# A depthwise convolution and a spiral scan on one core: PSUM seeded by ScalarE, half of the final updates split over ScalarE and GpSimd

## What is computed

```python
# layer 0
h = relu(x)
h = depthwise_conv3x3(h, dilation=2, SAME) + dw_bias
h = h @ pw + pw_bias                      # 256 -> 256
h = h * inv + (beta - moving_mean * inv)  # inv = gamma * rsqrt(var + 0.001)
# layer 1: one scan over the 3136 points of a spiral, from the centre outwards
for ci, neighbours in spiral:
    local = g[:, ci]
    neigh = mean of the (up to 4) neighbours' current values
    y = tanh(concat(local, neigh) @ w1 + b1) @ w2 + b2     # 512 hidden units, one scalar per image
    g[:, ci] = local + y * w_y
```

## Time and profile before

| | us |
|---|---|
| median of three runs | 4998.29 |
| the profiled execution, its own time | 5006.68 |
| its span | 5004.8 |
| PE busy | 4586.7 (92%) |
| DVE busy | 4012.3 (80%) |
| POOL busy | 3523.9 (70%) |
| ACT busy | 2289.1 (46%) |

### The profile page before, as it was taken

The page is one execution under the profiler, slowest core; times in us unless marked ns, Lnnn a source line. Parts: engine busy times, 40 slices in busy tenths (PEclk is TensorE's granted clock), DMA queues, the critical chain, the costliest instruction groups (busy, mean ns, idle before and its releaser), DMA issues.

```text
span 5004.8 us, 62963 instructions
## 1 busy us (share of the span) xinstructions
PE 4586.7 (92%) x20107; PEld 3278.7 (66%) x20107; DVE 4012.3 (80%) x6122; ACT 2289.1 (46%) x3670; POOL 3523.9 (70%) x2480
## 2 busy tenths in 40 slices
PE   3999999999999999999999999988888888887865
PEld 2778888888888888888888887744444444444432
DVE  6888888888887888888888888288888887877753
ACT  2555555555555555555555554343444443333321
POOL 3888888888887888888888888565666655554321
PEclk7999999999999999999999999999999999999985
DMA  3344344434444444343444342499998988876530
GB/s 92 112 131 138 128 138 128 138 128 138 128 138 131 135 128 138 128 138 128 138 128 138 128 138 106 173 315 295 295 313 285 285 271 253 242 222 188 168 108 25
DMA packets 395138, 835.35 MB, mean 167 GB/s; under 512 B 76864, under 2 KB 178496, under 8 KB 394688
## 3 DMA queue, kind: packets, MB, share of 16 engines
q1 hardware_dynamic: 251408, 420.08, 30.5%
q0 software_dynamic: 143408, 411.26, 22.0%
HBM read 419.95 MB, written 425.85 MB: 169 GB/s over the span
## 4 chain that ended last, share of the span: by engine, by line
PE 69%; DVE 11%; issue 11%; POOL 4%; ACT 3%; DMA 2%; SPq 0%; another core or an unknown queue 0%; POOLq 0%; DVEq 0%; ACTq 0%
PE psum L849 14%; PE psum L851 14%; PE psum L850 14%; PE psum L833 13%; PE psum L862 5%; DVE psum L706 4%; PE psum L820 3%; DVE dw_rows L714 3%; POOL out L463 2%; ACT psum L539 2%; PE psum L871 2%; PE psum L831 2%; PE psum L881 1%; DMA out<-dw_rows 1%; DVE near L706 1%
## 5 line engine op out<-in xcount | busy, mean ns | idle before, releaser
L631 DVE SCALAR_TENSOR_TENSOR dw_rows<-relu_rows,taps,dw_rows 128x1792 f32<-128x1792 f32 x872 | 1803.1, 2079 | 25.0 <-ACT dw_rows L516 19.7
L444 POOL DMA_INDIRECT s_x<-xo,wave_idx x784 | 1440.3, 1837 | 315.0 <-issue 213.1
L463 POOL DMA_INDIRECT out<-dw_rows x897 | 891.2, 993 | 870.7 <-DVE dw_rows L714 497.7
L849 PE MATMUL psum<-w_hi,u_hi 128*128 128x512 f32 x3136 | 1384.7, 442 | 0.0
L450 POOL DMA_INDIRECT s_pre<-eo,wave_idx x784 | 1170.3, 1493 | 246.7 <-issue 207.3
L851 PE MATMUL psum<-w_hi,u_lo 128*128 128x512 f32 x3136 | 1234.6, 394 | 0.0
L850 PE MATMUL psum<-w_lo,u_hi 128*128 128x512 f32 x3136 | 1221.1, 389 | 0.0
L481 ACT ACTIVATE eo<-psum 128x512 f32<-128x512 f32 x784 | 468.6, 598 | 1495.6 <-PE psum L851 1417.2
L862 PE MATMUL psum<-dw_rows,ident 128*128 128x512 f32 x1794 | 979.9, 629 | 165.3 <-DVE near L706 104.3
L539 ACT ACTIVATE psum<-psum 128x512 f32<-128x512 f32 x897 | 522.1, 582 | 916.7 <-PE psum L871 468.1
L706 DVE CUSTOM_DVE_ANT_0 psum<-psum,dw_rows,b_col 128x512 f32<-128x512 f32 x897 | 678.2, 756 | 204.6 <-ACT psum L539 145.8
(11 more groups left out here) (95 smaller groups left out, 3886.0 us busy)
## 6 DMA issues: line engine op xcount, KB each, us to landing
dw_rows<-s_pre SPq DMA_DIRECT2D x615, 256.0 KB
x_tok<-x SPq DMA_DIRECT2D x112, 896.0 KB
dw_rows<-s_x SPq DMA_DIRECT2D x615, 128.0 KB
dw_rows<-s_pre SPq DMA_DIRECT2D x169, 192.0 KB
dw_rows<-s_x SPq DMA_DIRECT2D x169, 96.0 KB
out<-dw_rows POOLq DMA_INDIRECT x897
s_x<-xo,wave_idx POOLq DMA_INDIRECT x784
s_pre<-eo,wave_idx POOLq DMA_INDIRECT x784
```

Source lines behind the costliest of these rows:

```text
L444: pool.indirect_dma_start(s_x, bass.IndirectOffsetOnAxis(wave_idx[:, n:n + 1], 0), xo[:, n % XO_SLOTS, :], None, bounds_check=TILES * P - ...
L463: pool.indirect_dma_start(out_rows, bass.IndirectOffsetOnAxis(store_idx[:, c:c + 1], 0), o_t[:, c % OUT_SLOTS, :], None, bounds_check=OUT_ ...
L631: dve.scalar_tensor_tensor(out=dst, in0=pair_rows(relu_rows, k + ky - 1, c, 2 * kx * NB), scalar=taps[:, c, 3 * ky + kx:3 * ky + kx + 1], ...
L849: pe.matmul(bank, hi, w_hi[:, k, :], start=k == 0, stop=False)
```

## The change

ScalarE fills PSUM where TensorE did, in both stages, and a part of the final updates leaves VectorE.

- Stage 1: the product L831 is gone. `bias_all` is the bias on all 128 partitions. ACT copies it into a bank at the end of its tick, behind the high part, centre tap or relu of that tick; PE's first L833 of tile n waits for this copy (`xp_filled`) and accumulates onto it.
- Stage 2: `hand_over` is now an ACT copy of 512 columns from SBUF into PSUM, ahead of the tanh of tile c. PE's `add_sums(c)` waits for it. Six products prime the banks once.
- Stage 2: for odd tiles ACT computes w_y times y into `prod` (2 slots) two tiles later, and POOL adds x (a `tensor_tensor` of 128x256) and then stores. Even tiles stay with DVE. POOL runs both kinds in the order of the tiles.
- In the setup, the chain that built `bias_rows` and `pick` is gone.

```diff
@@ sync
-                        sp.wait_ge(out_ready, c - XT_SLOTS + 1)
+                        sp.wait_ge(out_ready[c % 2], (c - XT_SLOTS) // 2 + 1)
@@ gpsimd
             for c in range(TILES):
-                pool.wait_ge(out_ready, c + 1)
+                if c % 2:
+                    pool.wait_ge(prod_ready, c // 2 + 1)
+                    pool.wait_ge(xt_in[c % XT_SLOTS], 16 * (c // XT_SLOTS + 1))
+                    if c >= OUT_SLOTS:
+                        pool.wait_ge(tile_out[c % OUT_SLOTS], 16 * (c // OUT_SLOTS))
+                    pool.tensor_tensor(o_t[:, c % OUT_SLOTS, :], prod[:, c // 2 % PROD_SLOTS, :],
+                                       x_t[:, c % XT_SLOTS, :], ALU.add).then_inc(out_ready[1], 1)
+                pool.wait_ge(out_ready[c % 2], c // 2 + 1)
                 pool.indirect_dma_start(out_rows, ...
@@ scalar, before the ticks
+            for n in range(XP_BANKS):
+                act.activation(xp_bank(n), bias_all[:, :], ACT.Copy).then_inc(xp_filled, 1)
@@ scalar, last in each tick
+                n = tick - ROW_AT - 1
+                if 0 <= n < TILES1 - XP_BANKS:
+                    act.wait_ge(xp_copied, n + 1)
+                    act.activation(xp_bank(n), bias_all[:, :], ACT.Copy).then_inc(xp_filled, 1)
@@ scalar, stage 2
+            def hand_over(c):
+                act.wait_ge(pre_in[c % PRE_SLOTS], 16 * (c // PRE_SLOTS + 1))
+                if c >= BANKS:
+                    act.wait_ge(y_ready, c - BANKS + 1)
+                act.activation(psum[:, c % BANKS, :], pre_t[:, c % PRE_SLOTS, :], ACT.Copy).then_inc(passed, 1)
+            def product(c):
+                level, g = SEQ[c]
+                act.wait_ge(y_ready, c + 1)
+                if c // 2 >= PROD_SLOTS:
+                    act.wait_ge(out_ready[1], c // 2 - PROD_SLOTS + 1)
+                act.activation(prod[:, c // 2 % PROD_SLOTS, :], wy_row, ACT.Copy,
+                               scale=hist[:, g, PAD + level:PAD + level + 1]).then_inc(prod_ready, 1)
             for c in range(TILES):
+                if c + AHEAD < TILES:
+                    hand_over(c + AHEAD)
                 act.wait_ge(pre_ready, c + 1)
                 act.activation(... ACT.Tanh).then_inc(th_ready, 1)
+                if c > 1 and c % 2:
+                    product(c - 2)
@@ vector
                 dot(c)
-                if c:
+                if c % 2:
                     finish(c - 1)
@@ tensor
-                    if n >= 2:
-                        pe.wait_ge(xp_copied, n - 1)
-                    bank = psum[:, 6 + n % 2, 0:C]
-                    pe.matmul(bank, pick[:, :], bias_rows[:, :], start=True, stop=False)
+                    pe.wait_ge(xp_filled, n + 1)
+                    bank = xp_bank(n)
...
-                pe.matmul(psum[:, c % BANKS, :], ident[:, :], pre_t[:, c % PRE_SLOTS, :], start=True,
-                          stop=False).then_inc(passed, 1)
+            for b in range(BANKS):
+                last = pe.matmul(psum[:, b, :], ident[:, :], v_rows[:, :], start=True, stop=True)
+            last.then_inc(primed, 1)
...
+                pe.wait_ge(passed, c + 1)
                 pe.matmul(psum[:, c % BANKS, :], s_rows[:, part, :], v_sel[:, row, :], start=False,
```

More of the change, by code:

```diff
@@ L28 @@
 PART_TILES = (4, 3)
+XP_BANKS = 2
 CONV_AT = 0
@@ L52 @@
 X_BEHIND = 4
+PROD_SLOTS = 2
 V_ROWS = 4
@@ L291, in build @@
         x_t = in_dw.take(XT_SLOTS * C).rearrange("p (k n) -> p k n", k=XT_SLOTS)
+        prod = in_dw.take(PROD_SLOTS * C).rearrange("p (k n) -> p k n", k=PROD_SLOTS)
         o_t = in_dw.take(OUT_SLOTS * C).rearrange("p (k n) -> p k n", k=OUT_SLOTS)
@@ L310, in build @@
         b1_r = su.take(HID)
-        brow, brow2 = su.take(C), su.take(C)
         be = su.take(HID)
@@ L324, in build @@
         lo_ready = sem("lo_ready")
+        xp_filled = sem("xp_filled")
         xp_ready = sem("xp_ready")
@@ L338, in build @@
         xt_in = [sem(f"xt_in{i}") for i in range(XT_SLOTS)]
+        primed = sem("primed")
         passed = sem("passed")
@@ L348, in build @@
         s_ready = sem("s_ready")
-        out_ready = sem("out_ready")
+        prod_ready = sem("prod_ready")
+        out_ready = [sem("out_ready_dve"), sem("out_ready_pool")]
         tile_out = [sem(f"tile_out{i}") for i in range(OUT_SLOTS)]
@@ L362, in near_sum, with xp_bank @@
             return near_slot(R // H, R % H - 1)[:, :, NB:NB + COLS]
+        def xp_bank(n):
+            return psum[:, 6 + n % XP_BANKS, 0:C]
         def part_cols(part):
@@ L430, in _ @@
             pool.memset(ident[:, :], 0.0).then_inc(setup_p, 1)
-            pool.memset(pick[:, :], 0.0)
-            pool.memset(bias_rows[:, :], 0.0)
             pool.memset(dw_rows[:, :, :, :], 0.0).then_inc(setup_p, 1)
@@ L486, in _ @@
                         act.wait_ge(x_stored[n % XO_SLOTS], 16 * (n // XO_SLOTS))
-                    act.activation(xo[:, n % XO_SLOTS, :], psum[:, 6 + n % 2, 0:C], ACT.Copy).then_inc(xp_copied, 1)
+                    act.activation(xo[:, n % XO_SLOTS, :], xp_bank(n), ACT.Copy).then_inc(xp_copied, 1)
                 R, n = row_at_tick(tick)
@@ L536, in _ @@
             last.then_inc(v_ready, 1)
+            act.wait_ge(primed, 1)
+            def hand_over(c):
[10 more added lines that the diff above has]
+                               scale=hist[:, g, PAD + level:PAD + level + 1]).then_inc(prod_ready, 1)
+            act.wait_ge(rows_in, 48)
+            for c in range(AHEAD):
+                hand_over(c)
             for c in range(TILES):
+                if c + AHEAD < TILES:
+                    hand_over(c + AHEAD)
                 act.wait_ge(pre_ready, c + 1)
                 act.activation(psum[:, c % BANKS, :], psum[:, c % BANKS, :], ACT.Tanh).then_inc(th_ready, 1)
+                if c > 1 and c % 2:
+                    product(c - 2)
                 for part, level in HIGH_ROWS_AT.get(c, ()):
@@ L544, in _ @@
                     act.activation(s_rows[0:96, part, :], psum[0:96, BANKS + part, 0:P], ACT.Copy).then_inc(hi_row, 1)
+            product(TILES - 2)
         @block.vector
@@ L569, in _ @@
             link(dve.tensor_tensor(cst, cst, bet, ALU.add))
-            dve.wait_ge(setup_p, 3)
-            for p in (0, 32, 64):
-                link(dve.memset(pick[p:p + 1, :], 1.0))
+            link(dve.tensor_copy(bias_all[:, :], cst))
             assert done[0] == SETUP_CST
@@ L715, in finish @@
                                          in1=x_t[:, c % XT_SLOTS, :], op0=ALU.mult,
-                                         op1=ALU.add).then_inc(out_ready, 1)
+                                         op1=ALU.add).then_inc(out_ready[0], 1)
             own_ops, in_ops = 0, 0
@@ L782, in _ @@
                     sum_rows(part, level)
+            assert TILES % 2
             finish(TILES - 1)
@@ L786, in _ @@
         def _(pe):
+            pe.wait_ge(setup_p, 3)
             pe.wait_ge(setup_v, SETUP_CST)
@@ L827, in _ @@
                     pe.wait_ge(conv_step, conv_done_for(R // 2))
-                    if n >= 2:
-                        pe.wait_ge(xp_copied, n - 1)
-                    bank = psum[:, 6 + n % 2, 0:C]
-                    pe.matmul(bank, pick[:, :], bias_rows[:, :], start=True, stop=False)
+                    pe.wait_ge(xp_filled, n + 1)
+                    bank = xp_bank(n)
                     for c in range(CK):
                         last = pe.matmul(bank, dw_rows[:, R % D_SLOTS, c, NB + P * t:NB + P * (t + 1)], pw[:, c, :],
-                                         start=False, stop=c == CK - 1)
+                                         start=False, stop=c == CK - 1, skip_group_check=True)
                     last.then_inc(xp_ready, 1)
@@ L888, in _ @@
             pe.wait_ge(cleared, 1)
-            for c in range(AHEAD):
-                hand_over(c)
             for c in range(TILES):
-                if c + AHEAD < TILES:
-                    hand_over(c + AHEAD)
                 add_sums(c)
@@ L933 @@
 N_W = 16
-SETUP_CST = 1 + 6 + CK + 3 + 3
+SETUP_CST = 1 + 6 + CK + 3 + 1
 SETUP_T = SETUP_CST + 4
-SETUP_V = SETUP_T + 2 * CK + 3 * CK + 3 + 2 + 1 + 1 + 2 + 1 + (1 + 6) + (1 + 3) + 1
+SETUP_V = SETUP_T + 2 * CK + 3 * CK + 3 + 2 + 1 + 1 + 2
 _INPUTS = ["x", "L0_conv_dw_kernel", "L0_conv_dw_bias", "L0_conv_pw_kernel", "L0_conv_pw_bias",
```

19 lines of the change are left out of this document (3 added, 16 removed).

## The result

| | us |
|---|---|
| median before, four runs beside those of after | 5001.78 |
| median after, four runs | 5199.35 (5188.74 to 5203.85) |
| ratio | 1.0392, 95% interval 1.037 to 1.0415 |
| profiled execution of after, its span | 5188.74, 5186.9 |

The change costs 197.6 us. Forecast were 92 more (5090 on 4998.3), with the same sign; the measured time lies at the upper end of the range of 4935 to 5200. The two profiled executions lie 182 us apart by their spans, since that of before was one of the longer runs of its kernel and that of after the shortest of its own.

What follows compares the result with a forecast made beforehand. PE was taken to pace stage 1 with POOL full as well, no engine full in stage 2, where POOL would become the bound. Terms -45 - 4 + 126 + 6 + 16 - 6 = +93 on 4998.3 gave 5090 us, range 4935 to 5200.

Steps and rivals of the forecast that it cites:

- the rival by which it hides the add: Rival (a), stage 2: store preparation overlaps POOL's add, or the add is near 0.31; 4930 to 4960 us, chance 0.18.
- rival (c): Stage 2 slower than forecast: DVE's finish waits for odd stores' landing, clock low throughout; up to 5230 us, chance 0.10.
- Seven to five groups: Stage 2, 577 tiles: POOL becomes the bound at 1.89 us a tile, 1090 us against 964, +126.
- the sum of 3.78 us for two tiles: POOL's stage 2 cycle: 0.97 + 0.70 + 0.79 + 0.97 + 0.30 = 3.73, with 0.05 for the shared port.
- Three and two groups: Stage 2: 1.2 GHz for part of the time, 0.25 us for each of 64 levels, +16; bounds 0 and 56.
- PE's part of the loop gets shorter: Stage 2: the loop over two tiles becomes shorter on PE and is taken over by the copy on ACT.
- Stage 1: 784 bias products removed, -94, waits on ACT's copy added, +49: -45 us, or -49 with the setup's -4.
- PE's wait for the relu's tick: Stage 1: PE waits once a row for ACT's bias copy behind the relu, 112 x 0.43 = +49 us.
- the 94 us: Stage 1: 784 bias products at 0.12 us, all on PE's pace, removed: -94 us.
- the bound that decided: Stage 1: gain 0 when POOL can't follow with its scatters; as rival (d), 5135 us, chance 0.08.
- A sign of being wrong: Stage 1: ACT waiting for the scatters' landing, listed among the signs that the prediction is wrong.
- One group: Stage 2, last stretch: half the finishes leave the chain, 16 x 0.40 = -6 us.

Runs made afterwards that it cites:

- The split alone: The whole change with the hand-over left on PE (5169.58 us) against the seeding alone (4970.05 us): 200 us.
- the filler: One PE product of identity and 512 zeros per tile added: to the whole change, 5160.21 us; to the kernel without the split, 4922.08 us.
- the kernel with PE's hand-over: The whole change, but with the hand-over left on PE as a product; bias seeding and split finish stay: 5169.58 us, ratio 1.0341.
- without the split: The change with ScalarE's hand-over, but every finish on DVE and no GpSimd add: 5092.84 us, ratio 1.0199.
- the seeding alone: Only the bias half of the change, against before: ScalarE seeds PSUM in stage 1, stage 2 as before: 4970.05 us, ratio 0.9945.

## Why the prediction was right or wrong

**Direction right, mechanism of the largest term right.** GpSimd became the bound, in the order and with the gaps that the sum names, and the rival by which it hides the add is out: the add measured 0.75 us, not 0.31, and the gap 0.80, not 0.30. The split alone costs 200 us. The time, though, lies above the forecast's own 5020 to 5180, where rival (c) stood with a chance of 0.10. Of (c)'s two reasons the clock holds and the wait for landings doesn't.

**Seven to five groups: mis-sized, +126 forecast, +167 measured.** The step that failed is the sum of 3.78 us for two tiles, which was 3.91. With the means of the stretch the parts are an add of 0.76 where 0.70 was taken, stores of 0.997 where 0.97 was, twice, and a gap of 0.80 for 0.79; together 3.86, or 0.08 more. The long adds (0.94 to 0.96 in place of 0.75) are in that mean: 20 of 287. The other 0.05 are gaps that no sum had: eleven of the gaps between add and store are longer than 0.85 us, five of them 3.47, and they hold 16.5 us beyond 0.80 each. This is one of them:

```profile
3424.28 0.75 POOL L472 TENSOR_TENSOR dw_rows<-dw_rows 128x256 f32<-128x256 f32 x1
3428.50 0.99 POOL L475 DMA_INDIRECT out<-dw_rows  x1 [3.47 <-issue]
```

The five stand at every 110th store, and the kernel with PE's hand-over has five as long at the same stores; what GpSimd waits for there no row shows. With 288 pairs 0.13 us make 37 of the 41 us.

**Four groups: +6 forecast, +13 measured.** It is the same cycle, 128 x 1.95; the filler leaves it at 250, and with PE's hand-over, clock up, it is 249.

**Three and two groups: +16 forecast, +57 measured.** This is the step that failed most for its size. The cause was right, the amount not: I took 1.2 GHz for part of the time, 0.25 of a possible 0.86 us for each of 64 levels. The clock was down nearly all through stage 2, and the filler puts the price at 0.8 us a level, 51 of the 57 us. The other 6 stay with the filler; the split does that, since with PE's hand-over three groups take 207 us where they take 199 without the split. The row of one group had shown the clock at 0.50 while PE still made its hand-overs; with about half of PE's work gone, as the prediction says itself, the case in which every step is at the slow level belonged in the sum, and not a third of it.

**What the sum left out.** With seven to five and four groups I gave the clock nothing, and there GpSimd hid it. Without the split it costs 1007 - 936 and 255 - 213 us there, and 164 in all of stage 2. The prediction's sentence that PE's part of the loop gets shorter was true only at 2.4 GHz. Rival (c), in which the clock cost 40, was the one that pointed this way, still too small.

**Stage 1: the right number for a wrong reason.** -49 was forecast and -48 read from the pair of profiles; the seeding alone gives -28 by the medians. The ten first dots of the same code lie 27 to 55 us ahead of that of before, so the 48 is one draw out of these. PE's wait for the relu's tick is there, but it isn't what is left of the 94 us. This is the wait in after, ScalarE's tick first and then PE:

```profile
2015.16 1.86 ACT L542 ACTIVATE relu_rows<-psum 128x896 f32<-128x896 f32 x1
2016.77 0.52 ACT L551 ACTIVATE psum<-bias_all 128x256 f32<-128x256 f32 x1
```

```profile
2017.44 1.10 PE L867 MATMUL psum<-pw,dw_rows 128*128 128x256 f32 x4 [0.18 <-ACT psum L551]
```

The relu ends at 2017.02, the copy 0.27 later, as in the sum, though it takes 0.52 us and not 0.38 (0.426 in the mean of all, over the upper bound of 0.42), because it starts earlier. PE starts 0.15 behind the copy, where 0.24 was worked out. In the 2820 us from 280 on PE waits so 103 times, once a row, with 0.29 us of idle time each and not 0.43. With all bias work gone the first dot is no earlier than here, so the bound that decided was the one that the prediction named and then passed over: GpSimd was full, and a part of the gain didn't show. A sign of being wrong that the prediction names did come: ScalarE waits for the scatters' landing, 67.6 us in after, where in before no such wait shows in these 2820 us. With a quarter of the scatters gone 115 us show (3250 - 3135); by the window above 133 instructions a row became 126, 26.9 us a row against 27.8, which is 0.128 us a tile and 100 us in all; the other 15 are within what first dots of the same code differ.

**One group: the right number, and the reason isn't borne out.** -6 was forecast for the finishes that leave the chain, -7 measured. But without the split, with ScalarE's hand-over, this stretch takes 174.5 us, as near to after's 173.4 as can be told, and with the split and PE's hand-over 181.3 against the 183.1 of the seeding alone. So the gain came with the hand-over that left PE, which has the low clock here in before too (0.61), and not with the finishes. The setup's -4 can't be told apart.

**The rest.** The steps give 41 + 7 + 41 us above the forecast of 93, which makes the 182 of the spans. The medians lie 15 further apart than the two profiled executions; which stretch holds those 15 no profile shows, though stage 1 differs by up to 28 us between profiles of kernels with the same code in it.

## What to carry to other kernels

Work that a change takes off TensorE can be what keeps its clock at 2.4 GHz: if the trace has a stretch where the clock is down, price every TensorE step in the chain at that level for the kernel after, as one case of the sum. On an engine that runs in order, look whether an instruction that is ready can stand between another and the one that waits for it: here the order add, next store, own store made the 0.80 us behind an add 0.17, and 0.5 us less for two tiles. It needed more buffers, which by themselves gave nothing. Where two engines are full at once, relieving one shows only as much as the other leaves. And before a difference of 20 us is given a cause, see how far kernels differ in a stretch whose code is the same: here by up to 28.

## What the runs showed of the hardware

- A GpSimd add took 762 ns for 256 fp32 columns and 369 ns for 64, in the mean of 287: 2.0 ns a column and 0.24 us besides. The most frequent lengths, 0.75 and 0.34 us, give 2.1 and 0.20.
- Between a GpSimd add and an indirect store that needs its result lie 0.80 us, much as behind a finish of DVE (0.79); an unrelated store behind an add starts after 0.17, and one behind another store after 0.30.
- GpSimd's add and DVE's instructions stretch each other. With seven to five groups in after, the 224 finishes that overlap no add take 0.49 us in the mean and at most 0.55; the 64 that overlap one take 0.77 and up to 1.41. Of the adds 20 took over 0.9 us in place of 0.75. This is DVE in after, a finish and a small product whose usual lengths are 0.48 and 0.19:

```profile
3302.96 0.48 DVE L748 SCALAR_TENSOR_TENSOR dw_rows<-dw_rows,near 128x256 f32<-128x256 f32 x1 [2.25 <-DMA out<-dw_rows]
3303.36 1.26 DVE L767 TENSOR_TENSOR near<-near,relu_rows 128x35 f32<-128x35 f32 x1
```

The product lasts until 3304.62, just past the end of GpSimd's add at 3304.56. The Trainium skill, page SBUF — State Buffer, section "SBUF: two separate sides", calls the pair of ports that the two engines share an exclusive lock, which whichever instruction starts first has until it ends. The ends of the two rows agree with a lock; their starts don't, since the product's row begins first. What held it between 3303.55, where its usual length would end, and the begin of the add's row at 3303.81 no row shows.

- A TensorE product that computes nothing (identity times zeros, one per tile) brought the granted clock of the kernel without the split from 0.54 to 0.99 with seven to five groups and made its stage 2 164 us shorter.
